# Decoder layer, attention stage: the last sums, the last stores and the second rows of maxima are issued in another order

## The reference, cut to what matters

```python
qkv = x @ qkv_w.T + qkv_b                       # for 4 batches of 1024 tokens
q, k, v = ...                                   # (4, 16, 1024, 16) each
q = apply_rotary(q, cos, sin)
k = apply_rotary(k, cos, sin)
attn = jnp.einsum('bhqd,bhkd->bhqk', q, k) * scale
attn = jax.nn.softmax(attn, axis=-1)            # the maximum of each row is taken first
out = jnp.einsum('bhqk,bhkd->bhqd', attn, v)
```

## Time and profile before

| | |
|---|---|
| median of 3 runs | 1169.53 us (1168.98 to 1169.67) |
| the profiled execution: its own time | 1170.64 us |
| the profiled execution: its span, first to last instruction | 1168.9 us |
| mean granted TensorE clock | 0.947 |
| PE busy | 1066.8 us (91%) |
| DVE busy | 1009.0 us (86%) |
| ACT busy | 767.8 us (66%) |
| Pool busy | 533.4 us (46%) |

### The profile page before, as it was taken

The page is one execution under the profiler, slowest core; times in us unless marked ns, Lnnn a source line. Parts: engine busy times, 40 slices in busy tenths (PEclk is TensorE's granted clock), DMA queues, the critical chain, the costliest instruction groups (busy, mean ns, idle before and its releaser), DMA issues. The chain is left out here.

```text
span 1168.9 us, 23162 instructions
## 1 busy us (share of the span) xinstructions
PE 1066.8 (91%) x8508; PEld 593.9 (51%) x8508; DVE 1009.0 (86%) x2108; ACT 767.8 (66%) x932; POOL 533.4 (46%) x866
## 2 busy tenths in 40 slices
PE   7988899999999999999999999988883069999998
PEld 6875433333333333333333333357773048888897
DVE  8998999999999999999999999437998975666653
ACT  4551288888888888888888888944555024555653
POOL 2647945454545363545444523232200023766665
PEclk8998599999999999999999999989997559999999
DMA  6787743232322334242424220055522022554443
GB/s 236 260 250 216 173 80 80 49 74 50 77 56 63 62 64 70 46 78 50 84 39 85 48 54 16 21 153 175 191 84 95 0 87 70 145 144 115 113 113 36
DMA packets 90140, 114.03 MB, mean 98 GB/s; under 512 B 31104, under 2 KB 62832, under 8 KB 90032
## 3 DMA queue, kind: packets, MB, share of 16 engines
q1 hardware_dynamic: 66872, 69.57, 20.5%
q0 software_dynamic: 19824, 36.48, 15.8%
q10 hardware_dynamic: 3336, 6.56, 1.6%
HBM read 73.31 MB, written 38.27 MB: 95 GB/s over the span
## 5 line engine op out<-in xcount | busy, mean ns | idle before, releaser
L835 DVE TENSOR_REDUCE b_max_halves<-banks 128x1 f32<-128x512 f32 x1024 | 625.1, 681 | 7.5 <-PE banks L882 7.5
L760 ACT ACTIVATE b_probs<-banks 128x1024 f32<-128x1024 f32 x512 | 520.4, 1027 | 110.8 <-PE banks L913 110.8
L882 PE MATMUL banks<-b_k,b_q 62*128 62x512 f32 x1024 | 391.9, 467 | 12.3 <-DVE b_max_halves L835 4.5
L913 PE MATMUL banks<-b_q,b_k 64*128 64x512 f32 x1024 | 378.8, 453 | 0.1
L898 PE MATMUL banks<-b_probs,b_v 128*17 128x256 f32 (+1 forms) x3840 | 314.3, 400 | 0.2 <-ACT b_probs L760 0.2
L913 PEld LDWEIGHTS banks<-b_q,b_k 64*128 64x128 f32 x1024 | 158.2, 185 | 228.6 <-issue 180.6
L882 PEld LDWEIGHTS banks<-b_k,b_q 62*128 62x128 f32 x1024 | 164.0, 189 | 38.3 <-DVE b_max_halves L835 33.6
L898 PEld LDWEIGHTS banks<-b_probs,b_v 128*17 128x17 f32 x3840 | 63.9, 95 | 164.8 <-issue 96.9
L572 POOL TENSOR_TENSOR b_att<-b_out,b_rec_spread 128x512 f32<-128x512 f32 x32 | 40.8, 1276 | 165.6 <-DMA b_rec_spread<-reciprocals 127.3
L1613 POOL DMA_INDIRECT e_x<-rows,d_idx x32 | 45.3, 1416 | 110.3 <-DVE d_wx L1788 56.8
L1833 DVE TENSOR_TENSOR e_hTl<-e_hT,e_hTh 128x512 fp32r<-128x512 f32 x64 | 47.8, 746 | 48.3 <-ACT e_hT L1587 48.3
(11 more groups left out here) (264 smaller groups left out, 1586.7 us busy)
## 6 DMA issues: line engine op xcount, KB each, us to landing
e_w<-in_w SPq DMA_DIRECT2D x16, 1024.0 KB, 7.6
q_stacks<-a_parts SPq DMA_DIRECT2D x32, 256.0 KB, 3.9
k_stacks<-a_parts SPq DMA_DIRECT2D x32, 256.0 KB, 4.2
b_q<-q_stacks POOLq DMA_DIRECT2D x60, 128.0 KB, 3.4
b_k<-k_stacks POOLq DMA_DIRECT2D x30, 256.0 KB, 4.9
v_tiles<-a_v ACTq DMA_DIRECT2D x8, 544.0 KB, 3.6
b_rec_spread<-reciprocals SPq DMA_DIRECT2D x128, 32.0 KB, 4.4
attended<-b_att SPq DMA_DIRECT2D x128, 32.0 KB, 2.4
```

The source lines that it names most:

```text
L760: nc.scalar.activation(pr[:, S % NP, u], ps[:, 2 * u:2 * u + 2, :], ACT.Exp, scale=D ** -0.5).then_inc(s_ex[u], 1)
L835: v.tensor_reduce(mxp[:, (k // NB) % 2, s, p, t, kh:kh + 1], ps[:, bank(k), :], AX.X, ALU.max)\
L882: nc.tensor.matmul(ps[:, bank(k), :], qs[g][stack, h, p, P * t:P * t + P], ks[g][stack, p, CH * kh:CH * kh + CH], start=True, stop=True).t ...
L913: return nc.tensor.matmul(ps[:, 2 * u + s, :], ks[g][stack, u, P * kt:P * kt + P], qs[g][stack, h, u, :], start=True, stop=True)
```

## The change

SP no longer stores pair 12 in the projection; that store joins the other three in `end_stores`, and `end_stores` moves behind the rows of n = 1. The rows of n = 1 are issued by two streams, stack 0 by SP and stack 1 by Pool. On Pool, `end_sums` waits for the first turn, and the loads of group 2 wait for the second turn and the rows that follow it. On ACT, `end_leading` moves behind the first rows. `ones(2)` and `ones(3)` move behind `tail.spread` of half group 1. The thresholds in `rows_in` follow the new counts.

```diff
@@ -188,6 +188,7 @@
                 nc.scalar.activation(whole(n, 0), summed[:], ACT.Copy).then_inc(s_end, 1)
 
         def end_stores(sp):
+            store_pair(sp, 2 * J - 4)
             sp.wait_ge(s_end, 6)
             store_pair(sp, 2 * J - 3)
             store_pair(sp, 2 * J - 2)
@@ -213,11 +214,9 @@
             sp.dma_start(cw["wp"][:], wts["wp"].rearrange("(k p) n -> p k n", p=P)).then_inc(s_wp, 16)
             sp.dma_start(cw["bp"][:], wts["bp"].partition_broadcast(P)).then_inc(s_wp, 16)
             sp.dma_start(bv[:], wts["bvqkv"]).then_inc(s_wp, 16)
-            for c in range(J - 1):
+            for c in range(J - 2):
                 sp.wait_ge(s_pb, 2 * c + 1)
                 store_pair(sp, 2 * c)
-                if c == J - 2:
-                    continue
                 sp.wait_ge(s_pb, 2 * c + 2)
                 store_pair(sp, 2 * c + 1)
                 if c == J - 5:
@@ -669,9 +668,9 @@
 
         def rows_in(eng, n):
 
-            eng.wait_ge(s_row[n % 2], 128 + 64 * (n // 2))
-            if n > 1:
-                eng.wait_ge(s_row2, 64 * n - 64)
+            eng.wait_ge(s_row[n % 2], 64 * (n // 2) + (64 if n % 2 else 128))
+            if n > 0:
+                eng.wait_ge(s_row2, 64 * n)
 
         def pair(k):
 
@@ -702,7 +701,6 @@
             sp.wait_ge(s_ra, 1)
             rows(sp, 0, 0, (0,))
             ones(1)
-            end_stores(sp)
 
             def body(i, first, last):
                 for hg in range(NH):
@@ -713,19 +711,22 @@
                     if not (last and hg == NH - 1):
 
                         sp.wait_ge(s_ra, NH * i + hg + 2)
-                        rows(sp, (hg + 1) // 2 % NG, (hg + 1) % 2, (0,) if back else (0, 1))
+                        rows(sp, (hg + 1) // 2 % NG, (hg + 1) % 2, (0,))
                     if not back:
-                        for g in range(2, NG):
-                            ones(g)
-                        sp.wait_ge(s_fill, 1)
+                        end_stores(sp)
                     if back:
                         tail.inverted(sp, m, x)
                     if hg > 1:
                         tail.store(sp, m - 1, i, (hg - 2) // 2, 1 - x)
                     elif not first:
                         tail.store(sp, m - 1, i - 1, NG - 1, 1 - x)
+                    if first and hg == 1:
+                        sp.wait_ge(s_fill, 1)
                     if back:
                         tail.spread(sp, m, x)
+                    if first and hg == 1:
+                        for g in range(2, NG):
+                            ones(g)
                     if last and hg == 3:
                         load_context_weights(sp, cw, s_cw, wts)
             bodies(sp, body)
@@ -759,9 +760,9 @@
                                 act.wait_ge(s_pv, 64 * i + S - NP + 1)
                             nc.scalar.activation(pr[:, S % NP, u], ps[:, 2 * u:2 * u + 2, :], ACT.Exp,
                                                  scale=D ** -0.5).then_inc(s_ex[u], 1)
-            end_leading(act)
             act.wait_ge(s_ra, 1)
             rows(act, 0, 0, (1,))
+            end_leading(act)
             bodies(act, body)
             take(NH * B - 1, 1)
 
@@ -782,9 +783,12 @@
                 clear_pad(g_, pool, ks[g], s_clear[g], 2)
                 if g == 1:
                     load(0, 1)
+                    pool.wait_ge(s_ra, 1)
                     end_sums(g_, pool)
                 if g == 2:
-                    pool.wait_ge(s_row[0], 128)
+                    pool.wait_ge(s_ra, 2)
+                    rows(pool, 0, 1, (1,), s_row2)
+                    rows_in(pool, 1)
                     load(0, 2)
             g_.memset(rb[:], 1.0).then_inc(s_fill, 1)
             pool.wait_ge(s_fill, 1)
```

## The result

The changed kernel takes 1171.99 us (median of 22 runs) against 1169.36 us for the kernel before (22 runs); the ratio is 1.0027, 95% interval 1.0016 to 1.0038. That is about 3 us slower, just beyond what was called no change, where the forecast was 1.8 us slower. The ratio leaves out one run of each kernel that lies far above all others (1308.87 and 1216.24 us), and so is not the ratio of the two medians. The profiled execution has a span of 1171.9 us.

A forecast was written before the change was run, and what follows sets the result against it. DVE's reduces, with almost no slack in attention, bound the kernel; 1170.64 - 0.9 - 2.5 - 0.8 + 4.3 + 1.7 = 1172.4 us profiled, median 1171.3 us, 8-in-10 range 1168.4 to 1175.0; chances: within 0.2% 0.53, slower 0.40.

The forecast's parts named there:

- The border: Start of attention: without pair 12's store the block opens earlier, PE limited by `b_v`; gain 0.9 us, between 0 and 2.28.
- Turn 0: First turn: Pool's sums no longer disturb it, so combine to turn takes about 0.63 instead of 3.16 us; gain 2.5.
- The cast: Second turn: the cast of `parts(1)` no longer meets Pool's memset; gain 0.76 us.
- Pool's list: Between turns 1 and 2: Pool's longer list delays `parts(2)`, so DVE waits at turn 2; loss 4.3 us.
- Pool goes on at 4.2: First item of Pool's list after turn 1: four rows issued by 2.6 us, landed 1.6 us later.
- The clock: PE stops about 4 us while DVE waits at turn 2, and the granted clock falls; loss 1.7 us, from 1.3 to 2.3.
- The stores on SP: Behind SP's rows after turn 1: sixteen stores take 17.8 to 20.1 us, finishing before turn 2; cost 0.
- The rival of SP coming late: Stores beside load 2 cost 1.5 us each, so rows land late for PE: 3.2 us more, 1174.5 us; chance 0.25.
- 0.5 late among SP's stores: Pool's rows before turn 2: if they land 0.5 us late, DVE's wait is 4.8 us instead of 4.3.
- The sum: Whole kernel: all gains and losses give 1172.4 us profiled, 1171.3 us median, which is +1.8 us or 0.15%.
- the likeliest case: Pool late at turn 2 and the clock low once; own range 1170.3 to 1172.6 us, chance 0.53.
- signs of being wrong: Turn 2 not released by Pool, PE waiting there for rows of maxima, or PE's first instruction much before 104.

The follow-up runs named there:

- e6: Changed kernel with one more wait: SP begins its sixteen stores only when Pool's four rows of n = 1 have landed; 1171.39 us, ratio 1.0018.
- e7: Changed kernel with 20 extra matmuls of 128 by 128 on PE while DVE waits at turn 2; 1170.03 us, ratio 1.0014.
- e1: Kernel before with only Pool's end_sums moved behind the first turn and ACT's end_leading behind the first rows; 1171.01 us, ratio 1.0036.
- e3: Changed kernel with Pool's memsets of pads 2 and 3 moved out of the stretch between turns 1 and 2; 1170.38 us, ratio 1.0028.
- e8: Changed kernel with load 2 back in its old place, ahead of the second turn and Pool's rows of n = 1; 1168.84 us, ratio 1.0014.
- e5: Changed kernel with load 2 and two of four store pairs before turn 1, sums split, Pool's list between turns 1 and 2 shortened; 1163.77 us, ratio 0.9958.
- e9: e5 with all eight rows of n = 1 issued by SP, as before the change; 1164.24 us, ratio 0.9965.

## Why the prediction was right, and where it was off

**The border**, 0.9 forecast: 1.1 between the two profiled executions (pause 3.96 to 2.85), some 0.7 over all kernels. After the change `b_v` releases PE, as said. Before it, it was the opening of the block: I had taken the row's releaser at its word, while `b_v` had landed 0.46 us earlier. Some 0.4 of the 1.1 is that opening; the rest is that `b_v` landed earlier, which differs from run to run.

**Turn 0**, 2.5: 3.16 to 0.62, that is 2.54. **The cast**, 0.76: 0.93 to 0.17, that is 0.76. Turn 1 came 4.43 us earlier where 4.2 was forecast.

**Pool's list**, 4.3: the loss from turn 1 to turn 2 was 5.74. Mechanism and place were right (DVE at turn 2, released by Pool's `parts`); the item that was too small is the first, "Pool goes on at 4.2": it measured 5.85. I had taken the 1.61 us from the landing of SP's rows. Pool's own rows began 0.42 later, and Pool went on 2.85 us after their issue ended instead of 1.61, which is 1.24 more; e6 shows that SP's stores make only 0.3 of it. The rest of the list was 0.2 shorter than forecast.

**The clock**, 1.7: 1.56, with 0.42 us lost for a microsecond of work at the low level where 0.43 was forecast; e7 keeps the clock up and the loss goes with it. The pause was 5.4 us, not about 4. The 3.1 to 5.3 us of low clock that the 1.7 is worked out from are the two stretches at 0.50 in the earlier trace rows; in the changed kernel it was some 3.7 us. One of the rows was read short: the 2.60 us without PE are the inside of a pause of 2.92 us. So the rows before showed 2.65 us with the clock kept at 1.00, and 2.92 and 4.12 with the clock lowered to 0.50.

**The stores on SP**: 17.8 us forecast, 14.9 measured, no cost in the changed kernel. The rival of SP coming late did not happen. But I counted only the time in which SP is busy issuing; what costs time in e1, e3 and e8 is the landing of small transfers behind large ones, 5.5 to 7 us instead of under 2. The prediction has for it only "0.5 late among SP's stores". More was not needed, because DVE's wait hid it, which is luck, and it would have been the term to know for anyone who shortens Pool's list.

The sum was +1.8 us, and at turn 3 the profiles differ by 2.87: 1.44 more on Pool's list, less 0.23 of larger gains and 0.14 of a cheaper clock. The median of 1171.99 us lies in the own range of the likeliest case (1170.3 to 1172.6). But by my chances no measurable change was likelier than slower (0.53 against 0.40), and by its ratio of 1.0027 the change ends on the slower side, with an interval that reaches down to 1.0016. None of the signs of being wrong showed: turn 2 is released by Pool, PE does not wait there for rows, and PE's first instruction comes at 103.48.

What the change gains shows in the rows: the sums behind the first turn, 2.5 us, and the cast, 0.8; the border, about 0.7, is no larger than its scatter. e5 and e9 keep these gains and come out 4 to 5 us below the kernel before by their ratios (4.8 at turn 3). What it loses comes from Pool's list between turns 1 and 2, load 2 and pad 3 behind the wait, and not from the second queue or the later `ones`, which e5 keeps. e8 shows that load 2 back in its place is not enough: its distance from the rows counts as well.

## What to carry to other kernels

When an engine has slack, look where in its list the slack stands: Pool had 8.48 us ahead of `parts(2)`, and moving a load of 7.1 us to the other side of one wait took the 7.4 us of memsets that stand behind it in the stream along, which spent all of it and 5.7 us more (the wait of DVE). A small transfer on which a critical engine waits is best issued when the large ones have landed or nearly so (Pool's rows took 1.7 to 2.7 us to land in e5, against 5.5 to 6.4 behind large transfers in e3 and e8); plan the large ones by when they have landed, not by when the queue has issued them (the last transfer of load 2 in e5 was issued by 140.48 and landed near 147.7). After one wait is removed, run again before believing in the gain: here twice the next wait stood right behind it and gave back all of it (e1 and e3).

## What the runs showed of the hardware

Transfers of 2 KB that land 1.7 to 1.8 us after their issue (Pool's rows at the third turn in the kernel before) took 5.9 to 6.4 us behind stores and loads under way (e3, Pool's rows) and 5.5 to 5.9 (e8), and SP's were there only 6.8 us after their issue had ended behind Pool's load 2 (e1), although the two are issued by different engines. In e9 one stream issues the eight rows in 5.26 us where the two of e5 need some 3 us (147.17 to 150.14), and turns 1 to 3 differ by at most 0.03 us from those of e5.

Twenty matmuls of 128 by 128 in the pause, with no idle time of PE left, kept the granted clock at 1.00; sixteen of 62 by 128, with 1.52 us left idle, did not, though PE counted as busy for 3.70 of 3.70 us with them. Nor does a PE that counts as busy run at the full clock for that: from 108 to 124 us in the kernel before, where PE does only `maxima` of 62 rows, it is busy for 16.00 of 16.00 us (28 matmuls) at a granted clock of 0.50.
